# Causal attention: jobs of a half in a mixed order of widths, 59 instead of 44 jobs ahead, another order of jobs, scores and sums

## The reference, cut to what matters

```python
qkv = (x @ W_qkv + b_qkv).reshape(b, s, 16, 24)      # 16 heads of 8
logits = einsum('bshd,bkhd->bhsk', q, k) / sqrt(8)
logits = where(k_pos > q_pos, -inf, logits)
attn = softmax(logits, axis=-1)
out = einsum('bhsk,bkhd->bshd', attn, v).reshape(b, s, 128) @ W_out + b_out
```

## Time and profile before

| | us |
|---|---|
| median of 3 runs | 1375.1 (1373.46 to 1375.84) |
| span of the profiled execution | 1375.5 |
| PE busy in it | 1322.9 |
| DVE busy | 1180.3 |
| ACT busy | 1009.6 |

### The profile page before, as it was taken

One profiled execution on the slowest core, in us unless ns is written; L12 is line 12 of the kernel. 1 busy time (PEld: TensorE's weight loads), 2 busy tenths in 40 slices (PEclk: granted clock), 3 DMA queues, 4 the chain that ended last, 5 costly groups with the idle time before them and its releaser, 6 DMA issues.

```text
span 1375.5 us, 26857 instructions
## 1 busy us (share of the span) xinstructions
PE 1322.9 (96%) x9681; PEld 679.7 (49%) x9681; DVE 1180.3 (86%) x2979; ACT 1009.6 (73%) x1791; POOL 142.5 (10%) x309
## 2 busy tenths in 40 slices
PE   9899999999999999999988987999999999999898
PEld 6444444444444444444435764555555555555487
DVE  7799999999999999999935987788888888888376
ACT  8678888888888888888883542677677776777743
POOL 5620000000000000000001211200000000000011
PEclk9699999999999999999998997899999999999999
DMA  7611101111101111101000333121112211120001
GB/s 212 189 32 32 30 4 32 32 32 33 28 7 32 33 33 32 30 6 31 2 1 1 110 106 93 33 59 38 34 33 49 48 33 34 41 56 3 3 24 39
DMA packets 40060, 58.44 MB, mean 42 GB/s; under 512 B 7796, under 2 KB 19448, under 8 KB 39928
## 3 DMA queue, kind: packets, MB, share of 16 engines
q1 hardware_dynamic: 39928, 56.72, 17.1%
HBM read 36.77 MB, written 18.87 MB: 40 GB/s over the span
## 4 chain that ended last, share of the span: by engine, by line
PE 84%; DVE 6%; ACT 5%; issue 3%; POOL 1%; DMA 1%; SPq 0%; DVEq 0%; POOLq 0%; ACTq 0%
PE psum L1160 28%; PE psum L1094 24%; PE psum L1126 16%; ACT probs L647 4%; PE psum L1022 3%; PE psum L1247 3%; PE psum L1231 2%; DVE maxima L876 2%; PE psum L1134 2%; PE psum L1176 1%; PE psum L1033 1%; DVE hid L952 1%; PE psum L1071 1%; PE psum L1007 1%; DVE junk L873 1%
## 5 line engine op out<-in xcount | busy, mean ns | idle before, releaser
L647 ACT ACTIVATE probs<-psum 128x512 f32<-128x512 f32 (+3 forms) x1386 | 832.3, 666 | 218.2 <-PE psum L1126 113.5
L876 DVE TENSOR_REDUCE maxima<-psum 128x1 f32<-128x512 f32 x1232 | 773.6, 682 | 33.3 <-PE psum L1094 27.8
L1094 PE MATMUL psum<-kop,qop 62*128 62x512 f32 (+3 forms) x1744 | 562.3, 437 | 7.5 <-DVE maxima L873 1.9
L1126 PE MATMUL psum<-qop,kop 64*128 64x512 f32 (+3 forms) x1792 | 522.0, 423 | 12.8 <-ACT probs L647 5.5
L1094 PEld LDWEIGHTS psum<-kop,qop 62*128 62x128 f32 x1744 | 267.2, 188 | 378.1 <-DVE maxima L876 285.6
L1160 PE MATMUL psum<-probs,v 128*32 128x512 f32 (+3 forms) x3584 | 441.9, 565 | 0.7 <-ACT probs L647 0.5
L1126 PEld LDWEIGHTS psum<-qop,kop 64*128 64x128 f32 x1792 | 266.8, 188 | 82.6 <-ACT probs L647 45.1
L873 DVE CUSTOM_DVE_ANT_0 junk<-psum,mask 128x384 bf16<-128x384 f32 (+3 forms) x512 | 232.2, 485 | 53.0 <-PE psum L1094 51.0
L1160 PEld LDWEIGHTS psum<-probs,v 128*32 128x32 f32 x3584 | 71.1, 109 | 100.8 <-issue 69.8
L1134 PE MATMUL psum<-half_ident,key_mask 64*128 64x64 bf16 x1024 | 88.8, 197 | 0.0
L540 POOL TENSOR_TENSOR att<-att_raw,rden 128x128 f32<-128x128 f32 x64 | 26.1, 407 | 512.5 <-DVE rden L905 512.5
(11 more groups left out here) (102 smaller groups left out, 751.6 us busy)
## 6 DMA issues: line engine op xcount, KB each, us to landing
qop<-q_parts SPq DMA_DIRECT2D x256, 64.0 KB
kop<-k_parts SPq DMA_DIRECT2D x64, 128.0 KB
kop<-k_parts SPq DMA_DIRECT2D x128, 64.0 KB
q_parts<-parts SPq DMA_DIRECT2D x24, 256.0 KB, 2.9
k_parts<-parts SPq DMA_DIRECT2D x24, 256.0 KB, 3.1
x<-in_L_attn_a_x SPq DMA_DIRECT2D x8, 256.0 KB, 4.0
q_parts<-att SPq DMA_DIRECT2D x8, 256.0 KB, 3.6
k_parts<-att SPq DMA_DIRECT2D x8, 256.0 KB, 3.6
```

The lines of the kernel that those rows point to most:

```text
L647: nc.scalar.activation(probs[:, slot, heads[0] % 2:heads[-1] % 2 + 1, c0:], psum[:, bank:bank + len(heads), c0:], ACT.Exp, scale=SCORE_SCA ...
L876: nc.vector.tensor_reduce(dst, src, AX_X, ALU.max).then_inc(ring_free, 1)
L1094: mm(psum[:, bank, 0:width], qop[rows, buf, f, r, qb * P:(qb + 1) * P].bitcast(F32R), kop[rows, buf, r, kh * CHUNK:kh * CHUNK + width].bit ...
L1126: ins = mm(psum[:, bank + k, c0:], kop[rows, buf, c // 2, j * P:(j + 1) * P].bitcast(F32R), qop[rows, buf, f, c // 2, c0:].bitcast(F32R), ...
```

## The change

The stream of a window's jobs gets an order written out by hand (`tiles`: head, block of queries, half of the keys), in which widths are mixed, but the jobs of half 0 still come before those of half 1. The string of the causal turn is another one, and 59 jobs go ahead instead of 44. Since 59 is more than the 48 of a window, the walk begins one turn earlier. `SHIFT_PAIR` is worked out from the walk and is 20 as before. The full layer's walk is the same. The first job of a window, which waits for the operands, is now whatever job the stream begins with. Every count of jobs, scores, sums and transposes stays.

```diff
--- before.py
+++ after.py
@@ -61,7 +61,7 @@
 
 
 
-    def __init__(self, causal, heads, unit_ring, job_ring, alternate, order, jobs_ahead, sums_behind, project_at, wide_step=99):
+    def __init__(self, causal, heads, unit_ring, job_ring, alternate, order, jobs_ahead, sums_behind, project_at, wide_step=99, tiles=None):
         self.causal, self.heads, self.unit_ring, self.job_ring = causal, heads, unit_ring, job_ring
         self.project_at = project_at
         self.wide_from = 10 ** 6
@@ -80,12 +80,17 @@
         for f in range(2):
             for qb in range(TPC):
                 width = (TPC * f + qb + 1) * P if causal else S
-                tiles = [(c, kh) for r in range(PAIRS) for kh in range(2) for c in (2 * r, 2 * r + 1)] if alternate \
+                in_head_order = [(c, kh) for r in range(PAIRS) for kh in range(2) for c in (2 * r, 2 * r + 1)] if alternate \
                     else [(c, kh) for c in range(HG) for kh in range(2)]
-                for c, kh in tiles:
+                for c, kh in in_head_order:
                     w = min(width - kh * CHUNK, CHUNK)
                     if w > 0:
                         stream.append((f, c, qb, kh, w, causal and kh * CHUNK + w == width))
+        if tiles:
+            found = {x[:4]: x for x in stream}
+            stream = [found.pop((f, *(int(d) for d in token))) for f in range(2) for token in tiles[f].split()]
+            assert not found
+        self.first_job = stream[0]
         self.last_of_half = [[x for x in stream if x[0] == f][-1] for f in range(2)]
         units = [(s, h) for s in range(n) for h in heads]
         assert order.count("j") == len(stream) and order.count("s") == len(units) and order.count("p") == n
@@ -94,7 +99,7 @@
         self.walk = []
         jobs = taken = 0
         last_unit = {}
-        for turn in range(-1, WINDOWS + 1):
+        for turn in range(-2, WINDOWS + 1):
             j, u, k = jobs_ahead, 0, -sums_behind
             for letter in order:
                 if letter == "j":
@@ -149,12 +154,13 @@
               order="jsjjsspjssjsjpjsjsjnsjjsspjssjsjpjsjsjsjjsspjssjsjpHjsjsjsjjsspjssjsjpjsjsjsjjsspjssjsjpjsjsjNsjjsspjssjsjpjsjsjsjjsspjssjsjphjsjsjsjjsspjssjsjpjsjs",
               jobs_ahead=48, sums_behind=2, project_at=(9, 11, 14), wide_step=5),
          Plan(causal=True, heads=PAIR_UNITS, unit_ring=2, job_ring=3, alternate=True,
-              order="sjjsjpjsjsjpjjjHsjjsjpjsjjspjjsjsjsjjnjjspjsjsjjpjsjjsjpjjsjsjpjjsjNjjsphjjspjjjspjjspjs",
-              jobs_ahead=44, sums_behind=1, project_at=(4, 6, 10))]
-
-
-SHIFT_PAIR = 20
-assert [item[0] for item in PLANS[0].walk].index("shift") in range(2 * SHIFT_PAIR - 3, 2 * SHIFT_PAIR + 1)
+              order="jjHjsjjsjjjspjssjjpjsjjsjspjjssjjpsjjpjssjjpjsjjsjpsjjjspjjssjjpjjsjspjjjhnNjjsjpjjssjjp",
+              jobs_ahead=59, sums_behind=1, project_at=(4, 6, 10),
+              tiles=("120 110 030 130 020 320 330 100 230 010 220 300 000 310 210 200",
+                     "310 121 311 100 030 300 211 200 321 031 201 230 110 231 120 210 221 330 021 001 320 010 301 331 111 000 101 011 131 220 130 020"))]
+
+
+SHIFT_PAIR = 2 * -(-[item[0] for item in PLANS[0].walk].index("shift") // 4)
 PE_JOBS_AHEAD, DVE_JOBS_AHEAD = 18, 22
 assert all(item[0] == "job" for item in PLANS[1].walk[:DVE_JOBS_AHEAD])
 
@@ -1087,7 +1093,7 @@
                 bank, buf = plan.job_bank + number % plan.job_ring, w % BUFS
 
                 wait(pe, ring_free, job_base + number - plan.job_ring + 1)
-                if (f, c, qb, kh) == (0, 0, 0, 0):
+                if job == plan.first_job:
                     earlier = layer * len(range(buf, WINDOWS, BUFS))
                     pe.wait_ge(operands_loaded[buf], (w // BUFS + earlier + 1) * LOADS)
                 rows, r = slice(TILE_ROWS * (c % 2), TILE_ROWS * (c % 2) + JOB_ROWS), c // 2
```

## The result

The changed kernel takes 1356.62 us (median of 4 runs, 1355.29 to 1357.66), the kernel before 1374.63 (1373.46 to 1375.84) beside it: a ratio of 0.9872, 95% interval 0.9858 to 0.9886. That is 18 us less, where 6 were forecast.

What follows compares the result with a forecast made beforehand. DVE's 3.6 us of idle time a turn behind PE's weighted sums was taken as the bound. Steady turns −9.1, fill +5.3, feed-forward jobs 0 and tail −2.4 gave −6.2 from 1375.5: 1369 us, range 1356 to 1386.

Steps and rivals of the forecast that it cites:

- the first turn pays the same: First causal turn: the clock is at 1.2 GHz in both kernels, so the half clock costs both the same there.
- the −0.4 for the last window: Last window: four jobs ahead of its first sum are gone, but ACT's four units hold it up anyway; −0.4 us.
- The fill: Before the first causal scores: 62 jobs instead of 44, more work than the shift's wait hides; +5.3 us, scores at 857.4.
- full cover: Rival for the causal turns: nothing is given back, −1.4 us a turn; −20 + 3 gives 1358 us; chance 0.17.
- What bounds the kernel: Causal turns: DVE's 3.6 us of idle time behind PE's weighted sums; DVE and PE hold each other up through three banks.
- The rule for idle time: Behind each sum: sum's length + 0.57 us + time from last job − DVE's three jobs ahead; 3.5 us a turn before, 2.15 after.
- Give-back at step 5: Scores of head pair 2 and 3 come before the first job behind step 5's sum; 0.25 us a turn lost.
- the bare count: Idle time behind each step by the rule alone, without give-backs; 2.15 us a turn, 0.34 or less except 0.58 and 0.37.
- Give-back for two transposes in a row: Behind step 8, a shift and both transposes of sums stand in a row, a further sum in effect; 0.5 us lost.
- The steady turns: Fourteen causal turns: DVE's idle time 2.9 instead of 3.55 us, busy time unchanged; −0.65 us a turn, −9.1 in all.
- The tail: End of the causal layer: jobs put ahead are missing, −2 us in turn 14, −0.4 in the last; −2.4 together.
- Same-half neighbours: Rival, slower: jobs next to each other on one half of PE's rows add 0.5 to 2.0 us a turn; chance 0.25.

Runs made afterwards that it cites:

- the relieved runs: Five kernels with DVE reading every second column of causal jobs over 128 columns and the causal exponential's scale a tenth; 1346.92 to 1365.84 us, one run each.
- e12: Changed kernel with jobs permuted within each half to make the idle-time rule's sum small; 1372.98 us, ratio 0.9993, turns 27.52 us.
- e3b: Changed kernel with half 1's 32 jobs in the old order by width, half 0's still mixed; 1375.23 us, ratio 1.0005, turns 27.99 us.
- e1: Changed kernel with the old order of jobs, new string and 59 ahead kept; 1407.94, 1430.03, 1430.58 and 3305.75 us, no ratio; turns 28.9 us at full clock.
- e2: Kernel before with the mixed order of jobs, old string and 44 ahead kept; 1420.54 us, ratio 1.033, profiled turns 29.94 us.
- e6: Changed kernel with one job moved ahead of the scores behind step 5's sums; 1359.63 us, ratio 0.9886, turns 26.91 us.
- e7: Changed kernel with one job put between the two transposes of sums; 1363.45 us, ratio 0.9908, turns 27.25 us.
- e4: Changed kernel with heads exchanged at the same widths, 6 same-half neighbours a turn instead of 27; 1358.15 us, ratio 0.9866, turns 26.93 us.
- e13: Changed kernel with jobs permuted within each half by a count following both PE and DVE; 1365.12 us, ratio 0.9935, turns 27.3 us.
- e10: Kernel before with nine added matmuls meant for the stop for the shift; the condition never held, so it is the kernel before again; 1374.72 us, ratio 1.0003.
- e8: Kernel before with an unread 128-column matmul behind each of jobs 18 to 43 and twelve in the stop for the shift; 1386.75 us, ratio 1.0082.
- e5: Changed kernel with heads exchanged at the same widths, 44 same-half neighbours a turn instead of 27; 1384.69 us, ratio 1.0057, turns 28.40 us.
- the searched order: Changed kernel's jobs permuted within each half to lower the idle-time rule's sum, here with DVE relieved; 1358.63 us in one run, turns 26.92 us.
- e18: Changed kernel with one job between the two transposes of sums and DVE relieved; 1355.81 us in one run, turns 27.01 us.
- e9: Changed kernel with an unread 128-column matmul behind each of jobs 18 to 61; 1385.59 us, ratio 1.010.

## Why the prediction was off

The direction was right, and the time lies in the range (near its low end), but the gain was three times the forecast. Three steps failed: the 0.75 us a turn of idle time that were to be given back at step 5 and behind the two transposes (DVE's idle time fell by 1.5 us a turn, not 0.65, while its busy time, put as fixed, rose by 0.4); "the first turn pays the same" for the half clock (−5.6 us); and the −0.4 for the last window (−5.1). The fill was put too low by 3.5 us. The rival "full cover" (1358 us) came nearest, in part by luck: its −20 us for fourteen turns were −19.9, but as −14.3 in thirteen turns and −5.6 in the first, which is mostly the clock; its +3 for fill and tail was +0.2.

- *What bounds the kernel*: half right. DVE's idle time of 3.6 us and its place were read rightly, and so was that DVE and PE hold each other up. The step "nothing else in the turn is nearer to a floor that no order can lower" was wrong. PE's 27.6 busy us were taken as modelled and thus as no bound; they too hang on the order, and the change lowered them by 0.8. How much of that is PE's work and how much short waits that modelled ends hide is open; the relieved runs show that with DVE idle for 10 us a turn the turns stay at 26.5 us or more, so something other than DVE's amount of work sets them there. ACT's ring, left out of the argument but for its busy time, was just under the surface.
- *The rule for idle time*: as a forecast of idle time it was good for the change, 2.15 us against 2.2 (0 to 3: 0.18, 0.01, 0.02, 0.02; the worst is step 5). As a measure of the turn it failed on e12, e3b, e1 and e2. It fitted before because it was made there.
- *Give-back at step 5* (0.25): idle behind step 5 is 0.82, 0.5 above the bare count, but steps 7 and 8 have 0.35 less; moving it (e6) gains nothing. *Give-back for two transposes in a row* (0.5): this term failed. Idle behind step 8 is 0.36, the bare count, and nothing behind the transposes, whose stretch DVE spends on two banked jobs and two reciprocals. DVE's timeline there, transposes of PE from 1045.64 to 1046.66:

```profile
1045.42 0.42 DVE L879 CUSTOM_DVE_ANT_0 junk<-psum,mask 128x256 bf16<-128x256 f32 x1 [0.32 <-PE psum L1100]
...
1045.77 0.69 DVE L879 CUSTOM_DVE_ANT_0 junk<-psum,mask 128x512 bf16<-128x512 f32 x1
...
1046.38 0.69 DVE L879 CUSTOM_DVE_ANT_0 junk<-psum,mask 128x512 bf16<-128x512 f32 x1
...
1046.99 0.36 DVE L911 RECIPROCAL rden<-att_raw 128x16 f32<-128x16 f32 x2
1047.29 0.56 DVE L879 CUSTOM_DVE_ANT_0 junk<-psum,mask 128x384 bf16<-128x384 f32 x1
```

  With its opposite (e7) the turn is 0.5 longer. Both terms out, the sum by the rule would have been −1.4 a turn, against −1.1 measured: near, but not for the rule's reason alone: 0.33 go with DVE's work, 0.76 stay without it, of which up to 0.5 is ACT's wait that the relief uncovered.
- *The steady turns*: 13 of them at −1.10 instead of −0.65, −14.3 against −8.4: −5.9 of the miss of 13.5 us. As means over these turns, DVE's idle time went from 3.69 to 2.21 us (−1.48 where −0.65 was forecast), and its busy time, forecast to stay, from 24.25 to 24.63. Of these 0.38 us 0.11 are longer records (29.94 to 30.05 us in sum), and the other 0.27 are records that reach less far into the next one: short delays of DVE that do not show as idle time, as in e12.
- *The fill*: +8.8, not +5.3. The first scores stood at 857.8 in e4, 859.2 in e13 and 860.9 here, and at 852.1 and 850.4 in two profiles of before, so some 1 to 3 us of it may be one execution's. In the changed profile PE stood 1.4 us for window 1's operands, at most 0.6 were allowed. From the 23rd job's reduction at 839.00 to these scores it took 21.9 us (21.0 to 22.1 in four others).

```profile
PE psum L1100 <- DVE maxima L879: 3.1, 6, 1.0
...
PE psum L1100 <- DMA kop<-k_parts: 1.4, 1, 1.4
```

- *"The first turn pays the same"* for the half clock: failed, and pays for the fill. The clock fell at 839 to 840 in both and rose at 873.4 in before, 867.7 here, while the scores came later. The excess over a turn is 6.9 us in before (7.4 in its second profile, e10) and 2.4 here, from one profile. e8 shows that this excess is the clock's and no other work of the first turn.
- *The tail*: turn 14 −3.5, of which 1.1 is the turn itself and 2.4 the missing jobs (2 forecast). The last window was put at −0.4 and gave −5.1 to the end. The runs with the new string have 92.5 to 92.6 there (e12 and e13, whose clock fell once at 1279 and 1273, 94.2), the old string has 96.2 in e2 and 96.5 in e8: about 3.8 us go with the string and the jobs ahead. Not all of that is work: e2 and e8 each have one stretch of 3.4 us at half clock there, both profiles of before have two (from 1289.8 and 1310.3 in the first; 97.64 in both), the new string has none but in e12 and e13. These falls come with the old string, and how much of the 5.1 us is theirs is not separated. I had taken ACT to hold that window up whatever PE does.
- *Same-half neighbours* (0.25 of the chance): right that they cost nothing for this change, but the reason does not hold: e5 lost 1.6 us a turn, at 0.1 each, while its jobs' loads stood 66.0 us behind DVE in ten turns, as long as in the changed kernel (66.8). A load that waits for DVE does not make a neighbour free.

The miss of 13.5 us again, measured less forecast: fill +3.5, first turn −4.9 (−5.6 for −0.65), turns 1 to 13 −5.9, turn 14 −1.5, last window −4.7. What stays open is which pairs within a half-height stretch cost PE its time (15.70 us against 16.21 in the searched order, with the same string), and how the waits for ACT and DVE share the rest in the kernels that are not relieved. No run enlarged a ring.

## What to carry to other kernels

When two engines hold each other up, a rule for one engine's idle time ranks orders only near the order from which it was taken; before trusting it, relieve that engine in a copy of the kernel and see how much of the difference stays. If an engine reads as 99% busy in a stretch and its ends are modelled, ask whether that time itself hangs on the order. A single half-height job between two full-height groups can cost as much as here, 0.5 us a turn at one place (e7, and with DVE relieved e18); where the order is free, put such groups behind each other.

## What the hardware showed that I had not expected

The clock: with half 0's jobs in the old order it fell to 0.5 for 6.8 us in every one of 14 turns, at the same place, with PE's records 98% busy (23.52 of 23.80 us at full clock, 6.63 of 6.80 at half). In the changed kernel it never fell in the causal layer behind 867.7. At the fill it stays at half for 27 to 44 us, with PE mostly busy from the first scores on, as in the earlier trace rows; with added matmuls and no gap in PE's records it stayed for 30.7 (e8) and 58.0 us (e9), against 34.1 in before. The Trainium skill (TensorE: Matmul & The Clock Gate, Part 1, What's actually happening) says that "the default state is throttled, and activity releases the throttle." Here records that read as busy were not enough to release it, and no run shows what was missing.
